# First step's two minima moved in among the projections, and three idle matmuls ahead of the first group's projections

## The reference

```
h = relu(layernorm(x))
q, k, v = h @ Wq.T + bq, h @ Wk.T + bk, h @ Wv.T + bv
mask[i, j] = graph(i) == graph(j)                  # 32 graphs of 64 rows; the last takes the rest
a = where(mask, q @ k.T / sqrt(256), 0)
scores = (a + adj + adj) * where(mask, 1, -1e6)
x = x + (softmax(scores) * mask) @ v
# second layer: a hyperbolic weighted mean with adj, x = x + expmap0(relu(logmap0(mean)))
```

## Time and profile before

| what | value |
|---|---|
| median of 3 runs | 778.23 us (777.74 to 779.25) |
| profiled execution | 782.14 us, span 780.2 us |
| busy: PE, DVE, ACT, POOL | 724.4 us (93%), 632.8 (81%), 474.9 (61%), 120.9 (15%) |
| mean granted TensorE clock | 0.972 of full speed |
| PE begins group 0, group 7, step 0's scores | 16.86, 68.29, 74.19 us of the span |
| POOL stages step 0's queries | 62.92 to 64.55 us |
| PE begins to weigh step 0's values | 97.04 us |

### The profile page before, as it was taken

One profiled execution on the slowest core, in us unless ns is written; L12 is line 12 of the kernel. 1 busy time (PEld: TensorE's weight loads), 2 busy tenths in 40 slices (PEclk: granted clock), 3 DMA queues, 4 the chain that ended last, 5 costly groups with the idle time before them and its releaser, 6 DMA issues.

```text
span 780.2 us, 14662 instructions
## 1 busy us (share of the span) xinstructions
PE 724.4 (93%) x4920; PEld 671.6 (86%) x4920; DVE 632.8 (81%) x1237; ACT 474.9 (61%) x870; POOL 120.9 (15%) x244
## 2 busy tenths in 40 slices
PE   5999699999999999999779899999999999999980
PEld 4988487888888888778779899999999999999980
DVE  6884677887778788879698888888888888888874
ACT  2553467777777799777554645555554455555853
POOL 3232211112221111285000000000000000000080
PEclk9999899999999999999899999999999999999995
DMA  4244686777677767777909699999899998988541
GB/s 143 80 135 183 224 312 250 291 288 261 245 256 277 289 252 277 277 190 157 214 19 221 142 213 202 202 194 188 188 190 208 200 192 184 191 191 186 122 162 59
DMA packets 52855, 157.11 MB, mean 201 GB/s; under 512 B 8640, under 2 KB 30272, under 8 KB 46656
## 3 DMA queue, kind: packets, MB, share of 16 engines
q1 hardware_dynamic: 52800, 156.47, 73.6%
HBM read 148.03 MB, written 8.42 MB: 201 GB/s over the span
## 4 chain that ended last, share of the span: by engine, by line
PE 42%; issue 29%; DVE 10%; POOLq 5%; DMA 5%; ACT 3%; DVEq 2%; POOL 1%; SPq 1%; ACTq 0%
PE bank L721 41%; DMA adjL<-in_adj 3%; DVE adjT_lo L1562 3%; DMA x_scratch<-x 1%; DVE turned L1554 1%; POOLq L622 1%; DVE bank L1554 1%; POOLq L642 1%; ACT adjT_hi L1066 1%; POOLq L628 1%; DMA w_raw<-in_L_gnn_Wk 1%; POOLq L572 1%; DVE X_lo L1542 1%; PE bank L713 1%; POOL q_low L580 1%
## 5 line engine op out<-in xcount | busy, mean ns | idle before, releaser
L721 PE MATMUL bank<-X_hi,adjT_hi 128*128 128x258 f32 x1024 | 292.5, 286 | 14.4 <-DVE adjT_lo L1562 14.4
L721 PE MATMUL bank<-X_lo,adjT_hi 128*128 128x258 f32 x1024 | 291.9, 285 | 0.0
L721 PE MATMUL bank<-X_hi,adjT_lo 128*128 128x258 f32 x1024 | 291.3, 284 | 0.0
L721 PEld LDWEIGHTS bank<-X_hi,adjT_hi 128*128 128x128 f32 x1024 | 195.6, 191 | 16.5 <-DVE adjT_lo L1562 14.1
L721 PEld LDWEIGHTS bank<-X_lo,adjT_hi 128*128 128x128 f32 x1024 | 195.9, 191 | 0.0
L721 PEld LDWEIGHTS bank<-X_hi,adjT_lo 128*128 128x128 f32 x1024 | 195.8, 191 | 0.0
L870 PE MATMUL bank<-values,probT 128*128 128x256 f32 x512 | 120.8, 380 | 1.4 <-ACT probT L1190 1.4
L1066 ACT CAST adjT_hi<-turned 128x1024 fp32r<-128x1024 f32 x64 | 67.0, 1048 | 69.5 <-PE bank L721 60.6
L870 PEld LDWEIGHTS bank<-values,probT 128*128 128x128 f32 x512 | 92.9, 189 | 14.8 <-ACT probT L1190 2.7
L1066 ACT CAST adjT_hi<-bank 128x1024 fp32r<-128x1024 f32 x64 | 64.9, 1014 | 63.9 <-PE bank L721 49.4
L1562 DVE TENSOR_TENSOR adjT_lo<-turned,adjT_hi 128x1024 fp32r<-128x1024 f32 x64 | 77.7, 1214 | 14.8 <-ACT adjT_hi L1066 14.8
(11 more groups left out here) (226 smaller groups left out, 1087.4 us busy)
## 6 DMA issues: line engine op xcount, KB each, us to landing
adjL<-in_adj SPq DMA_DIRECT2D x120, 512.0 KB, 8.5
adjU<-in_adj SPq DMA_DIRECT2D x32, 1024.0 KB, 7.7
adjL<-in_adj SPq DMA_DIRECT2D x16, 2048.0 KB, 7.8
x_scratch<-x SPq DMA_DIRECT2D x16, 258.0 KB, 3.2
xin<-in_x SPq DMA_DIRECT2D x8, 512.0 KB, 4.1
xt<-in_x SPq DMA_DIRECT2D x16, 256.0 KB, 6.4
adj<-in_adj SPq DMA_DIRECT2D x8, 512.0 KB, 13.4
x_all<-x_scratch SPq DMA_DIRECT2D x16, 256.0 KB, 10.8
```

Of the source, the lines that this page charges most:

```text
L721: last = pe.matmul(dst, a[i][a_cols], b[j][b_cols], start=(k_first and n == 0), stop=(k_last and n == 2))
```

## The change

Four edits. On PE, three products of `w_raw` into bank 7, which nothing reads before it is overwritten, stand between the folded biases and the first group. On ACT, the order within a projection group changes. On DVE, the decision on the path is taken after group 5; the two minima of step 0 are taken after groups 5 and 6 and kept in two columns of `mx`, and step 0 uses these; every later step takes its minima where it did. On POOL, step 0's lower block is marked as soon as the first `graph_row` copy and `adjL` are there, ahead of step 0's queries.

```diff
@@ buffers
-        up_bias = mx[:, HC:HC + 2]
+        up_bias, first_least = mx[:, HC:HC + 2], mx[:, HC + 2:HC + 4]
@@ POOL
-            pool.wait_ge(s_kq, KD * (NG // 2 + 1))
             pool.wait_ge(s_fast, 1)
...
+                pool.wait_ge(s_grow, 1)
+                mask_lower(step_at(0))
+                pool.wait_ge(s_kq, KD * (NG // 2 + 1))
                 stage_pair(step_at(0))
                 pool.wait_ge(s_grow, NG)
-                mask_lower(step_at(0))
                 pool.wait_ge(s_kq, KD * NG)
@@ PE
             folded_biases()
+            for _ in range(3):
+                pe.matmul(bank[7][:, 0:D], w_raw[:, 0, 0, 0:P], w_raw[:, 1, 0, :], start=True, stop=True)
             for g in range(NG - 1):
                 project(g, g % 2)
@@ ACT, project
                 queries(g, 0)
                 if g < NG - 1:
                     relu_h(g + 1, 1 - par)
+                queries(g, 1)
                 if g < NG - 2:
                     deviation(g + 2)
-                queries(g, 1)
+                act.wait_ge(s_grow_ps, g + 1)
+                act.copy(graph_row[:, g * CH:(g + 1) * CH], bank[2][:, :]).then_inc(s_grow, 1)
                 if g + 1 < NG // 2:
                     keys_lower(g + 1)
-                act.wait_ge(s_grow_ps, g + 1)
-                act.copy(graph_row[:, g * CH:(g + 1) * CH], bank[2][:, :]).then_inc(s_grow, 1)
@@ DVE
-            for g in range(NG):
+            for g in range(NG - 2):
                 project(g, g % 2)
...
-            dve.wait_ge(s_grow, NG)
+            dve.wait_ge(s_fast, 1)
...
+                def least_upper(s, to):
+                    dve.wait_ge(s_beside, 16 * s.n + 16)
+                    dve.tensor_reduce(to, adjU[:, 0:HALF], AX.X, ALU.min)
+                    return to
+                def least_lower(s, to):
+                    dve.wait_ge(s_adjL[s.par], turns(s))
+                    dve.wait_ge(s_pushed, s.n + 1)
+                    dve.tensor_reduce(to, adjL[:, s.par], AX.X, ALU.min)
+                    return to
...
-                    dve.wait_ge(s_beside, 16 * s.n + 16)
-                    dve.tensor_reduce(least[:, :], adjU[:, 0:HALF], AX.X, ALU.min)
+                    lowest = first_least[:, 1:2] if is_step(s, 0) else least_upper(s, least[:, :])
...
-                    dve.tensor_reduce(least[:, :], adjL[:, s.par], AX.X, ALU.min)
-                    maximum(s.par, 0, s_maxL)
+                    lowest = first_least[:, 0:1] if is_step(s, 0) else least_lower(s, least[:, :])
+                    maximum(s.par, 0, s_maxL, lowest)
...
+                least_upper(step_at(0), first_least[:, 1:2])
+                project(NG - 2, (NG - 2) % 2)
+                least_lower(step_at(0), first_least[:, 0:1])
+                project(NG - 1, (NG - 1) % 2)
                 scores_upper(step_at(0))
```

More of the change, by code:

```diff
@@ L655, in _ @@
             with pool.Else():
+                pool.wait_ge(s_kq, KD * NG)
                 def pair(s):
@@ L1748, in scores_lower, with maximum @@
                                              op1=ALU.mult).then_inc(s_qk_used, 1)
-                def maximum(par, slot, done, row=None):
+                def maximum(par, slot, done, lowest, row=None):
                     dve.drain()
-                    dve.scalar_tensor_tensor(out=top[:, :], in0=least[:, :], scalar=FAR, in1=top[:, :],
+                    dve.scalar_tensor_tensor(out=top[:, :], in0=lowest, scalar=FAR, in1=top[:, :],
                                              op0=ALU.mult, op1=ALU.max)
@@ L1766, in maximum_upper @@
                     dve.tensor_scalar(top[:, :], top[:, :], row, None, ALU.add)
-                    maximum(s.par, 1, s_maxU, row)
+                    maximum(s.par, 1, s_maxU, lowest, row)
                 def maximum_lower(s):
@@ L1855, in _ @@
             with dve.Else():
+                project(NG - 2, (NG - 2) % 2)
+                project(NG - 1, (NG - 1) % 2)
+                dve.wait_ge(s_grow, NG)
                 def pair(s):
```

## The result

The changed kernel takes 771.54 us (median of 4 runs, 768.65 to 772.95) beside 778.22 us of the kernel before (4 runs too): a ratio of 0.9904, interval 0.9877 to 0.9931, or 6.7 us.

The account below looks back on a forecast made before the run. PE was taken as the bound, losing time and clock mainly to a 5.33 us wait for DVE's step 0 minima. 5.0 + 0.9 - 0.7 = 5.2 us, from 778.23 to 773.0 us; own range 772.0 to 774.0, wide 770.2 to 776.0.

Parts of the forecast that it names:

- The minima: Step 0's two minima on DVE, moved among the projections: ACT's first copy at 91.4 instead of 96.40, gain 5.0 us.
- The delay taken for `adjL`: DVE's second minimum waits for `adjL` and POOL's mark: DVE 0.95 us late, about 0.8 us reaching the chain.
- ACT's exponentials are the next bound: After step 0's scores, ACT runs four exponentials back to back and is free at 91.3, setting the first copy.
- PE waiting 1.8 us: PE finishes the turned groups at 90.2 and waits for `probT` until its first weighing at 92.0.
- a sign of being wrong: The prediction is wrong if PE still waits for DVE at step 1's third column group.
- a wait of 1.8 us on PE does not lower it: No clock fall at PE's wait before its first weighing; the rival, a fall costing 2.0 us, had chance 0.22.
- ACT's order: Before group 3, PE no longer waits for ACT's `graph_row` copy: gain 0.9 us, bounds 0 and 0.9.
- The three matmuls: At PE's front, 2.7 us of products at full clock, partly repaid by earlier full clock: cost 0.7 us.
- a return of the clock 2.9 us earlier: At PE's front, unbroken work from 16.0 brings full clock back at 20.05 instead of 22.96.

Follow-up runs that it names:

- 5: The changed kernel run once more, nothing altered: 772.16 us, ratio 0.9915 to the kernel before.
- 11: The changed kernel with step 0's minimum over `adjU` back in its old place: 774.07 us, ratio 0.9939 to the kernel before.
- 6: The changed kernel with SP issuing `adjL` second, ahead of the right half of `adjU`: 772.20 us, ratio 0.9922 to the kernel before.
- 7: The changed kernel with `adjL` issued second and step 1's right half of `adjU` loaded in two quarters: 771.42 us, ratio 0.9913 to the kernel before.
- 8: The changed kernel with one idle matmul in place of three: 770.34 us, ratio 0.9905 to the kernel before.
- 10: The changed kernel with one matmul for three, `adjL` issued second, step 1's right half of `adjU` in quarters: 769.63 us, ratio 0.9881 to before.
- 12: The changed kernel with step 0's minimum over `adjL` back in its old place: 773.39 us, ratio 0.9937 to the kernel before.
- 1: The kernel before with only DVE's and POOL's part, the moved minima: 772.52 us, ratio 0.9913 to the kernel before.
- 4: The changed kernel without the three matmuls: 772.13 us, ratio 0.9902 to the kernel before.
- 9: The changed kernel with one idle matmul in place of three, a second time: 771.41 us, ratio 0.9900 to the kernel before.
- 2: The kernel before with only ACT's new order: 778.14 us, ratio 0.9971 to the kernel before.

## Why the prediction was right

**The minima (forecast 5.0).** Right. The trace's 5.4 us lie on it, and the changed kernel's second stretch of 28.67 us is what the working gave (91.4 less 62.90, 28.5). The delay taken for `adjL`, 0.8 us, was right for the execution profiled and zero for others; both ends of the bound (0 and 0.95) occurred. What made DVE late was the landing and POOL's mark, as argued.

**"ACT's exponentials are the next bound", with PE waiting 1.8 us.** The first half held to 0.2 us, the second failed: PE waits 0.24 us for `probT` at 89.36. The prediction let step 1's scores run unbroken from 83.0 to 89.2 and checked only the left half of step 1's `adjU` behind them. Their right half was never asked about: it is issued when step 0's scores have been read and landed 4.9 us later, and either PE waits for it (1.37 us) or the half clock covers it (5). This is what the prediction itself named as a sign of being wrong, that PE still waits for DVE at step 1's third column group. So PE and ACT come to the first copy within 0.2 to 0.5 us of each other, and 11 shows the forecast picture only once ACT is made 2.2 us later. That the copy still came where the working had it is partly luck: the load that was not asked about happened to end level with ACT.

**The clock.** That a wait of 1.8 us on PE does not lower it, read off one row, was wrong as a rule: behind the same wait, now 1.94 us, the clock fell in 5 and not in the first trace of the same kernel. Over all eleven traces with a moved minimum it fell within 0.5 to 1.5 us of that wait's end in seven (5 to 8, 10 to 12) and not in four (changed, 1, 4, 9).

**ACT's order (0.9).** Right: 1.0 to 1.1 in the traces, 1.0 to 3.5 timed.

**The three matmuls (-0.7).** This is the mis-sized term. Six records were priced at 2.7 us at full clock by the 3.75 us of eight. But eight records of the same shape take 2.00 us at 89.36, and 3.66 us at 91.06 in experiment 11, where the granted clock is 0.50 to 0.61. So the row used ran at about half rate, and six records cost at most 1.5 us at full clock (0.25 each by the row at 89.36). In 12, where the clock fell only at about 17.06, they took 1.23 us from start to start:

```profile
15.91 1.79 PE L767 MATMUL bank<-w_raw 128*128 128x256 f32 x6
17.14 0.99 PE L724 MATMUL bank<-hT_hi,wT_hi 128*128 128x512 f32 x1
```

In the changed kernel they ran at half clock for the most part, 2.15 us from start to start. The other half of the term, a return of the clock 2.9 us earlier, came, but 1, 2 and 4 show that it comes without them. What is left, in executions with a short slow stretch: 52.7 us to group 7 on the mean of six traces with the three, 51.8 of two without (2 and 4), a cost of 0.8; with ACT's old order it is 53.48 and 52.94, a cost of 0.5. The timed runs say otherwise: alone they gain 0.2 to 2.3 us, and 4 stands level with the changed kernel. The granted clock of those runs goes the same way: 0.9748 on the mean of 23 runs of before, 0.9777 on that of 12 with the three alone, which would be worth about 2.3 us (an estimate, 0.0029 of 777 us). But with the other parts in, the clock rises over before by 0.0059 without the three (4) and by 0.0052 with them (5). An explanation would be that the kernel before has the long slow stretch often and the one with three matmuls never; against it, 1, 2 and 4 have the short one too. Single traces can't tell, and the sign of this term stays open.

**The sum.** 5.2 us were forecast and 6.6 to 6.7 measured. 5.4 + 1.0 of the traces make 6.4 without the third part.

## What to carry to other kernels

When work is taken off the path, list every transfer that the next step reads, each half with its own issue, before naming the next bound. Price an instruction from rows that ran at a known clock, and check the row against the same shape elsewhere. A clock fall seen in one execution is no term of a sum: see whether it recurs in a second trace before crediting an edit with its end.

## What the runs showed of the hardware

- The granted clock of a stretch can read 1.00 while matmuls run at about half rate: 9 to 10 us of the changed kernel reads 1.00 below, yet its products there take 3.75 us for eight records, near the 3.66 at 0.50 to 0.61 in experiment 11 and not the 2.00 at 89.36. No fall had been recorded before that time.

```profile
9.00:10.00 1.00, 1.00 (x4) 0.73 (x4) 1.00 (x4) 0.00 (x0) 0.00 (x0) 1.00 1.04 356
```

- The same 2 MB load of `adjL`, issued in the same order, took 13.5 to 16.3 us to land in the eleven traces where it stood third, and 10.6 to 12.5 us in the three where it was issued second.
- The same wait of 1.94 us was followed by no fall of the clock in one execution and by a fall to 1.2 GHz 0.5 us after its end in another, of one kernel.
